# Hats made and stored three bands ahead, turns two bands ahead between the pairs of samples, and the spreads of the hats issued by GpSimd

## What is computed

```
x = x + gate_block(group_norm(x))        # per row: (a @ b), a sigmoid gate, three products by 128 x 128
x = x + deformable_conv(group_norm(x))
deformable_conv(z):
    z      = relu(z)
    offset = conv3x3(z, w_off) + b_off   # 18 channels: (dy, dx) for each of 9 taps
    sample = bilinear(z at base + offset), for 9 taps and all channels
    return einsum(sample, w_def)         # a 3x3 convolution over the samples
```

## Time and profile before

| | us |
|---|---|
| median of 3 runs | 1771.32 |
| the profiled execution | 1764.54 |
| its span, first to last instruction | 1762.7 |
| TensorE busy (matmuls) | 1562.9 |
| VectorE busy | 1103.9 |
| ScalarE busy | 974.2 |
| GpSimd busy | 939.1 |
| granted TensorE clock, mean | 0.976 |

### The profile page before, as it was taken

The page is one execution under the profiler, slowest core; times in us unless marked ns, Lnnn a source line. Parts: engine busy times, 40 slices in busy tenths (PEclk is TensorE's granted clock), DMA queues, the critical chain, the costliest instruction groups (busy, mean ns, idle before and its releaser), DMA issues.

```text
span 1762.7 us, 28712 instructions
## 1 busy us (share of the span) xinstructions
PE 1562.9 (89%) x10451; PEld 1150.9 (65%) x10452; DVE 1103.9 (63%) x1908; ACT 974.2 (55%) x1474; POOL 939.1 (53%) x734
## 2 busy tenths in 40 slices
PE   5999999538889999999999989899999899999998
PEld 3787777416666666666666656666666666666665
DVE  6888888625666666555565655656666565565653
ACT  3555555335556655565655655555655566655552
POOL 2555556326555665565565555555565555556552
PEclk9999999759999999999999999999999999999999
DMA  4343343235656666666666666666666666666652
GB/s 141 101 122 114 112 123 106 97 136 209 205 202 208 223 224 217 218 226 224 216 223 219 222 212 209 218 210 226 220 239 209 227 218 218 219 213 220 207 208 89
DMA packets 146137, 337.09 MB, mean 191 GB/s; under 512 B 10697, under 2 KB 77796, under 8 KB 146020
## 3 DMA queue, kind: packets, MB, share of 16 engines
q1 hardware_dynamic: 131620, 309.58, 51.6%
q10 hardware_dynamic: 14400, 25.96, 4.2%
HBM read 273.54 MB, written 61.95 MB: 190 GB/s over the span
## 4 chain that ended last, share of the span: by engine, by line
DMA 46%; POOL 16%; PE 15%; issue 13%; DVE 5%; SPq 3%; ACT 2%; POOLq 0%; ACTq 0%; DVEq 0%
DMA hx_all<-hat_x 41%; POOL weights L1550 10%; PE bank L745 5%; PE pair L717 4%; POOL x_bo L1504 4%; SPq L532 3%; DMA hat_x<-hats 3%; PE pair L790 2%; DVE hats L1280 1%; ACT dist L948 1%; DMA raw<-x_pad 1%; POOL rstd L1478 1%; PE bank L763 1%; POOL xT_lo L1491 1%; PE pair L728 1%
## 5 line engine op out<-in xcount | busy, mean ns | idle before, releaser
L1550 POOL TENSOR_TENSOR weights<-hy_all,hx_all 120x512 f32<-120x512 f32 x576 | 761.7, 1350 | 636.4 <-DMA hx_all<-hat_x 630.1
L745 PE MATMUL bank<-weights,zT 120*128 120x216 f32 (+1 forms) x2816 | 610.5, 347 | 29.2 <-POOL weights L1550 25.2
L745 PEld LDWEIGHTS bank<-weights,zT 120*128 120x128 f32 x2816 | 508.4, 192 | 109.5 <-POOL weights L1550 44.2
L1293 DVE SCALAR_TENSOR_TENSOR samples_lo<-bank,samples_hi 128x432 f16<-128x432 f32 (+1 forms) x704 | 401.8, 590 | 260.5 <-ACT samples_hi L963 253.1
L963 ACT ACTIVATE samples_hi<-bank 128x432 f16<-128x432 f32 (+1 forms) x704 | 364.5, 519 | 296.6 <-PE bank L745 284.3
L717 PE MATMUL pair<-samples_hi,w_hi 128*128 128x512 f16 x576 | 220.2, 382 | 0.9 <-DVE y L1328 0.9
L921 ACT ACTIVATE z<-raw,norm_band 128x690 f32<-128x690 f32 (+2 forms) x128 | 204.9, 1603 | 26.1 <-DMA raw<-x_pad 24.1
L717 PE MATMUL pair<-samples_lo,w_hi 128*128 128x512 f16 x576 | 219.1, 380 | 0.0
L717 PE MATMUL pair<-samples_hi,w_lo 128*128 128x512 f16 x576 | 219.0, 380 | 0.0
L763 PE MATMUL bank<-ident,z 128*120 128x128 f32 x640 | 106.8, 281 | 80.6 <-DVE zT L1314 80.6
L973 ACT COPY zT<-pair 120x512 f32<-120x512 f32 x192 | 112.1, 584 | 75.2 <-DVE hats L1280 43.4
(11 more groups left out here) (144 smaller groups left out, 2079.7 us busy)
## 6 DMA issues: line engine op xcount, KB each, us to landing
hy_all<-hat_y SPq DMA_DIRECT2D x192, 600.0 KB
hx_all<-hat_x SPq DMA_DIRECT2D x192, 600.0 KB
raw<-x_pad SPq DMA_DIRECT2D x68, 276.0 KB, 15.6
x_pad<-hy_all SPq DMA_DIRECT2D x64, 276.0 KB, 3.7
weights<-in_x SPq DMA_DIRECT2D x64, 256.0 KB, 2.9
out<-y SPq DMA_DIRECT2D x64, 256.0 KB, 15.6
hat_x<-hats ACTq DMA_DIRECT2D x64, 216.0 KB
hat_y<-hats ACTq DMA_DIRECT2D x64, 180.0 KB
```

What stands on the lines that cost most here:

```text
L745: mm = nc.tensor.matmul(sampled_pair(b)[:, :, at:at + BR * cols], zT[0:WPIX, u, w, :], weights[0:WPIX, u, :, w * WC * BR:(w * WC + cols) * ...
L1293: nc.vector.scalar_tensor_tensor(out=samples_lo[:, u, :, c0:c1], in0=sampled_pair(b)[:, :, 0:c1 - c0], scalar=PIXEL_SCALE, in1=samples_hi[ ...
L1550: nc.gpsimd.tensor_tensor(weights[0:WPIX, u, tap, :], hy_all[0:WPIX, k, :], hx_all[0:WPIX, k, :], ALU.mult).then_inc(weights_ready, 1)
```

## The change

Four things, all in the second block:

- The order of the work is another, and the prologues are gone: the list is walked from iteration -3 on. Hats (O, Q, the split of the offsets and the store) run three bands ahead instead of two, turns two bands ahead instead of one, and the turns stand between pairs of samples. The zT buffer of band n + 2 is the one that band n is sampled from, so the copy of a turn group waits for the pairs that read its windows (`pairs_until`).
- Steps that were one have letters of their own: h (the cast z_hi and the split z_lo), P (the split of the offsets), G (the hats), R (the maximum).
- There are three DRAM buffers of hats instead of two (`AHEAD = 3`).
- The spreads are issued by GpSimd, between its products: after the three products of a group it waits for its own last product and for the hats to have landed, and issues the two spreads of that group for the next band.

```diff
+AHEAD = 3
-        hat_rows = [nc.dram_tensor("hat_y", [2, TROWS, SRC_R, CHUNK], F32, kind="Internal").ap(),
-                    nc.dram_tensor("hat_x", [2, TROWS, SRC_C, CHUNK], F32, kind="Internal").ap()]
+        hat_rows = [nc.dram_tensor("hat_y", [AHEAD, TROWS, SRC_R, CHUNK], F32, kind="Internal").ap(),
+                    nc.dram_tensor("hat_x", [AHEAD, TROWS, SRC_C, CHUNK], F32, kind="Internal").ap()]
...
+        def pairs_until(n, g):
+            return PAIRS * n + min(2 * g + 2, PAIRS)
...
         ORDER = [(step[0], int(step[1:])) for step in (
-            "k0 O0 s0 s1 s2 Q0 k1 T0 k2 s3 H0 T1 T2 k3 s4 T3 s5 T4 k4 T5 c0 s6 c1 z0 k5 s7 "
-            "c2 c3 z1 k6 s8 c4 c5 k7 s9 c6 k8 s10 c7 c8").split()]
+            "z0 s0 c0 s1 k0 T0 z1 s2 c1 k1 s3 T1 h0 k2 c2 s4 s5 O0 T2 k3 c3 P0 s6 k4 c4 s7 T3 Q0 "
+            "c5 k5 G0 s8 c6 k6 H0 s9 R0 T4 k7 c7 s10 T5 k8 c8").split()]
...
+        def hats_landed(n):
+            return hat_out[n % AHEAD], 32 * (n // AHEAD + 1)
...
-        def bands(eng, stages, prologue):
-            prologue()
-            def band(n, u):
-                for kind, j in ORDER:
-                    ahead = {"c": -1, "s": 0, "k": 1, "T": 1, "O": 2, "Q": 2, "H": 2, "z": 3}[kind]
-                    if not 0 <= n + ahead < BANDS:
-                        continue
-                    if kind in stages:
-                        stages[kind](n + ahead, (u + ahead) % 2, j)
-            for n in range(BANDS + 1):
-                band(n, n % 2)
+        def bands(eng, stages):
+            ahead = {"c": -1, "s": 0, "k": 1, "T": 2, "z": 3, "h": 3, "O": 3, "P": 3, "Q": 3,
+                     "G": 3, "H": 3, "R": 3}
+            for n in range(-AHEAD, BANDS + 1):
                 for kind, j in ORDER:
+                    m = n + ahead[kind]
+                    if kind in stages and 0 <= m < BANDS:
+                        stages[kind](m, m % 2, j)
...
             for n in range(BANDS + 2):
...
-                if n + 2 < BANDS:
-                    spread_hats(n + 2, n % 2)
...
 # ScalarE (z_hi now in a step of its own), VectorE
+            def cast_z(n, u, _):
                 act.wait_ge(z_ready, n + 1)
                 wait(act, off_done, n)
                 nc.scalar.activation(z_hi[:], ...
...
-                if g == 0:
-                    wait(act, sampled, PAIRS * (n - 1))
+                wait(act, sampled, pairs_until(n - 2, g))
...
 # GpSimd
+            def spread_hats(n, g):
+                if n == BANDS:
+                    return
+                wait(pool, weights_ready, TAPS * (n - 1) + TROWS * (g + 1))
+                pool.wait_ge(*hats_landed(n))
+                rows = [hat_rows[0][n % AHEAD, g].rearrange("(o r) c -> o r c", o=1),
+                        hat_rows[1][n % AHEAD, g, g:g + NEAR_C].rearrange("(r o) c -> r o c", o=1)]
+                for dst, src in zip((hy_flat, hx_flat), rows):
+                    pool.dma_start(dst[g * SRC_R:(g + NEAR_C) * SRC_R,
+                                       g * CHUNK:(g + 1) * CHUNK],
+                                   src.broadcast_to([NEAR_C, SRC_R, CHUNK])
+                                   ).then_inc(hat_in[g], 16)
+
             def weigh(n, u, k):
+                if k % TROWS == 0 and n + k > 0:
+                    spread_hats(n + (k > 0), (k // TROWS - 1) % TROWS)
                 if k % TROWS == 0:
                     pool.wait_ge(hat_in[k // TROWS], 32 * n + 32)
...
+            pool.wait_ge(hats_cleared, 2)
+            for g in range(TROWS):
+                spread_hats(0, g)
+            bands(pool, {"k": weigh})
```

More of the change, by code:

```diff
@@ L799, in offsets @@
                 convolve_offset_parts().then_inc(off_done, 1)
-            def prologue():
-                pe.wait_ge(select_set, SELECT_STEPS)
-                pe.wait_ge(scaling, W_STEPS)
-                offsets(0, 0, 0)
-                for g in range(TGROUPS):
-                    turn_windows(0, 0, g)
-                locate(0, 0, 0)
-                offsets(1, 1, 0)
-                locate(1, 1, 0)
-            bands(pe, {"c": conv, "Q": locate, "s": sample, "T": turn_windows,
-                       "O": offsets}, prologue)
+            pe.wait_ge(select_set, SELECT_STEPS)
+            pe.wait_ge(scaling, W_STEPS)
+            bands(pe, {"c": conv, "Q": locate, "s": sample, "T": turn_windows, "O": offsets})
             pe.wait_ge(far_step, 1)
@@ L926, in make_z @@
                     scale=norm_band[:, 0].rearrange("p b n -> p (b n)")[:, n:n + 1])
-                if half == 0:
-                    return
-                done.then_inc(z_ready, 1)
+                if half == 1:
+                    done.then_inc(z_ready, 1)
+            def cast_z(n, u, _):
                 act.wait_ge(z_ready, n + 1)
@@ L974, in copy_windows @@
                                bank[B_ZT[0]][0:WPIX, 0:c * P]).then_inc(zT_a, 1)
-            def prologue():
-                act.wait_ge(select_set, SELECT_STEPS)
-                act.wait_ge(scaling, W_STEPS)
-                act.wait_ge(final, FINAL_STEPS)
-                for half in range(2):
-                    make_z(0, 0, half)
-                evict_offsets(0, 0, 0)
-                for half in range(2):
-                    make_z(1, 1, half)
-                for g in range(TGROUPS):
-                    copy_windows(0, 0, g)
-                distances(0, 0, 0)
-                evict_offsets(1, 1, 0)
-                store_hats(0, 0, 0)
-                distances(1, 1, 0)
-                store_hats(1, 1, 0)
-                for half in range(2):
-                    make_z(2, 0, half)
-            bands(act, {"Q": distances, "H": store_hats, "s": copy_samples, "T": copy_windows, "z": make_z,
-                        "O": evict_offsets}, prologue)
+            act.wait_ge(select_set, SELECT_STEPS)
+            act.wait_ge(scaling, W_STEPS)
+            act.wait_ge(final, FINAL_STEPS)
+            bands(act, {"Q": distances, "H": store_hats, "s": copy_samples, "T": copy_windows,
+                        "z": make_z, "h": cast_z, "O": evict_offsets})
         @block.vector
@@ L1277, in make_hats, with reach_of @@
                 dve.wait_ge(dist_ready, n + 1)
-                if not isinstance(n, int) or n > 0:
-                    dve.wait_ge(hat_out[1 - u], landed(n - 1, 1 - u, 32))
+                if n > 0:
+                    dve.wait_ge(*hats_landed(n - 1))
                 nc.vector.tensor_scalar(hats[:], dist[:], -1.0, 0.0, ALU.add,
                                         ALU.min).then_inc(hats_ready, 1)
+            def reach_of(n, u, _):
+                dve.wait_ge(dist_ready, n + 1)
                 nc.vector.tensor_reduce(farthest[RAW_AT:CONST_AT, bass.ds(n, 1)],
@@ L1334, in add_x1 @@
                 added.then_inc(y_ready, 1)
[L1336 to L1354 removed]
+            dve.wait_ge(scaling, W_STEPS)
+            bands(dve, {"c": add_x1, "P": split_offsets, "G": make_hats, "R": reach_of,
+                        "s": copy_samples_lo, "T": copy_windows, "h": split_z})
             dve.wait_ge(reached, BANDS)
@@ L1551, in weigh @@
                                         hx_all[0:WPIX, k, :], ALU.mult).then_inc(weights_ready, 1)
-            def prologue():
-                for k in range(TAPS):
-                    weigh(0, 0, k)
-            bands(pool, {"k": weigh}, prologue)
+            pool.wait_ge(hats_cleared, 2)
+            for g in range(TROWS):
+                spread_hats(0, g)
+            bands(pool, {"k": weigh})
 def kernel(x, L0_conv_Wa, L0_conv_ba, L0_conv_Wb, L0_conv_bb, L0_conv_Wg, L0_conv_bg, L0_conv_Wo,
```

41 lines of the change are left out of this document (4 added, 37 removed).

## The result

The changed kernel took 1810.7 us (median of four runs, 1807.6 to 1815.0) beside 1768.9 us for the kernel before in the same comparison: a ratio of 1.0245, interval 1.0205 to 1.0285. It is slower by 2.4%; the forecast was 1735. The profiled execution has a span of 1806.3 us.

A forecast was written before the change was run, and what follows sets the result against it. TensorE's list was taken as the bound: 18.8 us plus stalls 0.5, 0.7 and 0.6 make 20.6 a band. 429 + 1215 + 25 + 55 + 4 = 1728, plus 1.8 is 1730; median 1735, range 1690 to 1850.

The forecast's parts named there:

- Turns: TensorE's turns, moved between pairs of samples: their stalls on zT copies go, 1.0 us a band.
- locate: TensorE's locate, now some 3.6 us behind the offset products: its stall on the split offsets goes, cost put at nothing.
- c0 waits for y: Tap c0, now right behind s0, waits for y of the band before: a new stall of 0.5 us a band.
- Offset products wait for z_lo: TensorE at O0: a stall of 0.7 us a band from ScalarE's list, plus 0.6 for z_lo's collision with GpSimd.
- full collision: z_lo on VectorE lengthened by GpSimd's work by 1.07 us at most; in each band it gives the 21.1 us bound.
- The start: Without the old prologue: first weights near 389 us and y of band 0 near 429, 8 us earlier than before.
- rival A: GpSimd becomes the bound if an issue exceeds 1.4 us (forecast 1.1); at 1.9, 1906 us; chance 0.25.
- rival B: Spreads keep to the same ten engines on GpSimd's queue: about 21.3 us a band, 1776 us, no change; chance 0.17.
- the 20.6 us that I had read as nearly a second bound: DMA side: from issuing one band's six spreads to the last group's products starting, 20.6 us, nearly as long as a band.
- Rival C: Holes only move: ScalarE's z0, z1, z_hi delay sample copies, border at its upper bound: 1765 to 1790 us; chance 0.13.
- Border and end: Five image-border bands wait for raw blocks, 5 us each, 25 in all; the end, y(59) to y(63), takes 55 us.
- the side that had a chance of 0.25: Slower than 1789 us: rival A and the upper end of Rival C, chance 0.25.

The follow-up runs named there:

- the tiny DMAs: New order with spreads on SP, plus two 64-byte DMAs issued by GpSimd ahead of each group of products: 1787.7 us, ratio 1.0112.
- the two with late issues: Changed kernel with spreads issued behind k5 and k8: 1818.6 us; the same issues behind k5, with ten raw blocks and later offset products: 1852 us.
- the three kernels on SP with ten blocks: New order, spreads on SP, ten raw blocks instead of nine: 1700.0 us; offset products two steps later too: 1687.9; c0 behind s1 as well: 1664.7.
- the fill: New order with spreads on SP, plus GpSimd waiting for its last product and filling a scratch tile (0.95 us) before product groups: 1728.8 us.

## Why the prediction was wrong

**Turns: right; locate: only in part.** The waits of turns on copies are gone. Locate waits for offs_lo 7 times, 10.3 us in all, against 13 times and 14.5 us before: it never had the 1.5 us a band that the prediction left to it.

**c0 waits for y: right.** 31.5 us in 63 bands, 0.5 each, as worked out. What TensorE loses is a little more: the idle time listed begins at the modelled end of a product, 0.38 us behind its start, where the next would have started after 0.22. So 0.16 is to be added to each wait, here and below.

**Offset products wait for z_lo: the step that failed.** The text put 0.7 for ScalarE's list and "a little over half, 0.6" of a collision with "1.07 us more at most". The first part was right: with the spreads on SP, in the 26 of 54 bands in which z_lo isn't held, TensorE is idle for 0.57 us before the offset products, 0.73 lost. The second has the wrong bound: 1.07 was what one product adds, taken from a trace in which GpSimd issues no DMA. With issues directly ahead of its trains VectorE waits for up to three products. z_lo is held in all 54 bands, by 1.18 us on average, above the "full collision", with a single one at 4.2. TensorE is idle for 1.70 us, 1.86 lost, instead of 1.3: the collision costs 1.1 and not 0.6.

That is half of the 1.05 us by which a band is longer than forecast. The rest: 0.15 more for the wait on y, 0.14 idle a band for locate on offs_lo, which the prediction put at nothing, and the granted clock. Six of the 54 bands have a mean clock of 0.93 and take 23.5 us, the 48 others take 21.4, which makes 0.23 a band. TensorE is idle for 2.8 us in those six and 2.3 in the others; I take the dips as a consequence of the waits but didn't isolate them. The layout by hand was right and its price list was that of another GpSimd.

Windows of the changed kernel, a band of 23.2 us and the next of 20.9 (columns: window, us, busy us and instructions of PE, PEld, DVE, ACT, POOL, then granted clock, DMA share, GB/s):

```profile
554.70:577.90 23.20, 20.69 (x126) 14.99 (x124) 14.28 (x21) 12.63 (x20) 14.69 (x16) 0.93 0.79 218
577.90:598.80 20.90, 19.13 (x125) 14.23 (x125) 13.83 (x22) 12.55 (x20) 14.74 (x16) 1.00 0.78 213
```

**The start: wrong by 19 us.** The sum counted GpSimd's waits for hats only against products that come later. In the start there is nothing to spare: the issue for band 1 blocks the second group of band 0 for 10.9 us. With the spreads on SP, y of band 0 comes at 431.0, 2 us from the forecast of 429.

**GpSimd's issue, rival A: not so.** 0.59 us on average instead of 1.1, with 1.4 as the deciding point; its list is 9 x 1.27 + 6 x 0.59 = 15.0 us a band, and GpSimd waits for TensorE. The page named in that rival was nearer to the matter than my use of it: the Trainium skill (SBUF — State Buffer, "Who interferes with whom") says that VectorE's operations with two inputs in SBUF, and its copies and casts on both ports, share one pair of ports with GpSimd, and that whichever begins first holds it for the whole instruction. I looked for the victim on GpSimd's side, where five issues waited 8.5 us in all; it was VectorE. "For the whole instruction" agrees with every kernel without issues in GpSimd's list (least time plus at most 1.2 us, one product); behind an issue the trace shows the whole train of three, 3.98 us for a cast of 0.43, and the measurement decides.

**Ten engines, rival B: not so.** The plateau of 0.64 has become a mean of 0.79 over a whole band, and the two spreads of a group land in 6.2 and 8.8 us (medians). By the page of the Trainium skill cited there (DMA: Bandwidth & Descriptors, "Why a DMA increments its semaphore by 16 and not by 1") all 16 engines signal such a DMA, whatever its shape; that says nothing of how many carry it. The share is above ten sixteenths, so more than ten engines are at work; whether on one DMA or ten each on several in turn, it doesn't tell. The bytes don't move faster: 218 GB/s at 0.79 in the first window above, 215 at 0.64 in the earlier trace rows. And nothing was to be won, since the 20.6 us that I had read as nearly a second bound wasn't one: with the spreads on SP the kernels above run their bands in 20.5, 20.2 and 19.8 us on average. The span of the earlier trace rows held waits for room, not only transfers.

**Rival C (the holes only move, 1765 to 1790): nearest in kind.** They moved from zT to z_lo. It gave ScalarE as the reason; it was VectorE against GpSimd, and the time went past its upper end.

**Border and end: right,** 24 for 25 and 52 for 55 us.

Within the range of 1690 to 1850 the time fell on the side that had a chance of 0.25. The first kernel with the spreads on SP took 1732 us, near the forecast of 1735, which was in effect that of the change without its last part. That it comes so near is in part luck: 20.50 us a band for 20.6, a border of 33 us for 25, a first y at 431 for 429 and an end of 52 for 55 cancel.

## What to carry to other kernels

Before DMA issues move to GpSimd, list VectorE's operations that have two inputs in SBUF or are wide copies and casts (here z_lo, offs_lo, offs_hi and the hats), and ask of each what a delay of a whole group of GpSimd's instructions would do; behind an issue the delay wasn't bounded by one instruction here. If the issues must stay, let each of GpSimd's instructions behind them wait for the one before: that won back 42 of 78 us. A DMA issue that waits for a semaphore blocks all compute behind it on the same list (538.4 us in one kernel here), so what it waits for must be done earlier by more than the longest landing, at the start too. Split a change that has several parts before judging it: here one part gained 2.1% and the other cost 4.5%, and the gaining one, carried on, reached 5.9%.

## What the runs showed that was not expected

With a DMA issue directly ahead of a train, even one of 64 bytes, the three products run in 3.73 us and nothing interrupts them; z_lo and offs_hi take up to 5.06 and 3.98 us in the changed kernel, offs_lo up to 4.9 where the issues come late. Counted over operations of VectorE (z_lo, offs_hi, offs_lo, hats) that began in the first or second product of a train, those that ended only behind its third:

- The train starts within 0.1 us of an issue: 81 of 81 in the changed kernel, 63 of 63 with k3 behind z_lo, 89 of 89 with c0 behind s1, 65 of 65 with the tiny DMAs, 64 of 64 in the old order with spreads on GpSimd, 18 of 22 and 33 of 36 in the two with late issues.
- GpSimd stands idle for 0.3 us or more between the issue and the train: 0 of 6.
- No issue ahead: 3 of 85 in the kernel before, 1 of 52 with the spreads on SP, 5 of 124 in the three kernels on SP with ten blocks, 0 of 28 and 1 of 12 in the two with late issues, 0 of 11 with the fill.
- An issue ahead, but each product waits for the one before: 0 of 96.

Where GpSimd issues nothing, products are 1282 to 1350 ns long on average, against 1274 in the changed kernel, and z_lo and offs_hi wait for 1.2 us at most. Why an issue has this effect is open. Open too is a hole of 2.09 us ahead of a second issue (at 695.07); four issues have one of this length, and a short fifth makes it 8.5 us in all.

An issue by GpSimd took 0.56 to 0.62 us here, against 0.78 on SP; the price that was feared most was the smallest.
